# Recurrence of a hybrid kernel: VectorE's scan inputs ahead of sorting and placing, and GpSimd's scatters one step later

## What is computed

```python
# recurrence, for the normalised x of a batch; in time t the state is h
k = x @ Wz + bz
z = sigmoid(k)                                   # keep = 1 - z
h[t] = keep[t] * h[t-1] + z[t] * g(x @ Wh + bh)  # the reference does it in logs
out = layernorm(h) * gamma + beta + x
# mixture of experts, for the normalised rows xf
probs = softmax(xf @ router_w.T)
topv, topi = top_k(probs, 2)
y = sum over the two chosen experts of share * expert(xf)
```

## Time and profile before

| what | value |
|---|---|
| median of three runs | 1427.84 us (1422.67, 1434.9, 1427.84) |
| span of the profiled execution, first to last instruction | 1524.2 us |
| recurrence in that execution, first memset to the next stage's first load | 973.4 to 1238.1 us |
| roots of steps 8 to 35 (start to start) | 1025.27 to 1208.60 us |

### The profile page before, as it was taken

The page is one execution under the profiler, slowest core; times in us unless marked ns, Lnnn a source line. Parts: engine busy times, 40 slices in busy tenths (PEclk is TensorE's granted clock), DMA queues, the critical chain, the costliest instruction groups (busy, mean ns, idle before and its releaser), DMA issues. The chain is left out here.

```text
span 1524.2 us, 38116 instructions
## 1 busy us (share of the span) xinstructions
PE 1216.6 (80%) x11689; PEld 1017.3 (67%) x11689; DVE 1144.1 (75%) x3833; ACT 967.7 (63%) x2078; POOL 991.9 (65%) x1131
## 2 busy tenths in 40 slices
PE   5889999999999999973788888577787449888850
PEld 3667777777777777753788888455566348788850
DVE  5489999999999999965566665488888546666638
ACT  3588888888888888851555544277777435455420
POOL 4346688888888888777355665237777835666530
PEclk9699999999999999995799997588878669999955
DMA  7211111111111111123222222112222122222228
GB/s 199 86 46 46 48 60 60 60 60 60 59 60 60 60 60 60 39 93 83 73 86 86 81 85 68 49 49 83 73 83 69 45 68 84 86 84 84 77 83 277
DMA packets 99443, 117.19 MB, mean 77 GB/s; under 512 B 17784, under 2 KB 79792, under 8 KB 99248
## 3 DMA queue, kind: packets, MB, share of 16 engines
q1 hardware_dynamic: 70560, 73.57, 16.3%
q0 software_dynamic: 16896, 35.16, 6.8%
q10 hardware_dynamic: 11792, 6.05, 1.4%
HBM read 47.56 MB, written 41.51 MB: 58 GB/s over the span
## 5 line engine op out<-in xcount | busy, mean ns | idle before, releaser
L1153 DVE TENSOR_TENSOR ebuf<-score_banks,region 128x768 f32<-128x768 f32 x256 | 243.6, 951 | 18.8 <-PE score_banks L862 13.1
L1402 ACT ACTIVATE region<-ebuf 128x768 f32<-128x768 f32 x256 | 215.9, 860 | 23.0 <-DVE ebuf L1153 23.0
L1380 ACT CAST copied<-max_banks 128x768 bf16<-128x768 f32 x251 | 201.9, 804 | 15.1 <-PE max_banks L850 12.5
L1842 POOL DMA_INDIRECT choice_rows<-second_yo,second_xg x136 | 133.1, 979 | 112.7 <-PE second_by L1880 69.3
L1842 POOL DMA_INDIRECT choice_rows<-first_yo,first_xg x136 | 130.7, 961 | 114.0 <-PE first_by L1880 65.9
L1694 POOL DMA_INDIRECT expert_rows<-d_rows,a_d_index x112 | 129.4, 1155 | 27.9 <-issue 17.2
L1918 ACT ACTIVATE second_silu<-second_bgu,second_biases 128x256 f32<-128x256 f32 (+1 forms) x144 | 61.0, 466 | 114.3 <-PE second_bgu L1871 66.7
L1918 ACT ACTIVATE first_silu<-first_bgu,first_biases 128x256 f32<-128x256 f32 (+1 forms) x144 | 61.9, 462 | 111.8 <-issue 83.6
L1954 DVE SCALAR_TENSOR_TENSOR second_hT<-second_bgu,second_biases,second_silu 128x256 f32<-128x256 f32 (+1 forms) x144 | 62.1, 464 | 70.3 <-ACT second_silu L1918 37.6
L905 PE MATMUL bankO<-region,vaug 128*32 128x256 f32 (+1 forms) x2048 | 111.1, 334 | 1.9 <-ACT region L1402 1.9
L853 PE MATMUL max_banks<-region_r 32*128 32x256 f32 x502 | 98.3, 388 | 11.9 <-DVE ebuf L1153 7.4
(11 more groups left out here) (369 smaller groups left out, 4531.6 us busy)
## 6 DMA issues: line engine op xcount, KB each, us to landing
region_r<-region_r SPq DMA_DIRECT2D x192, 128.0 KB
first_xg<-expert_rows SPq DMA_DIRECT2D x64, 132.0 KB
second_xg<-expert_rows SPq DMA_DIRECT2D x64, 132.0 KB
z_rows<-choice_rows SPq DMA_DIRECT2D x32, 256.0 KB
c_rows<-choice_rows SPq DMA_DIRECT2D x16, 512.0 KB
out<-xres ACTq DMA_DIRECT2D x16, 256.0 KB
choice_rows<-first_yo,first_xg POOLq DMA_INDIRECT x136
choice_rows<-second_yo,second_xg POOLq DMA_INDIRECT x136
```

What stands on the lines that cost most here:

```text
L1153: nc.vector.tensor_tensor(ebuf[:, half_of_ebuf(c, j), :, :], score_banks[:, :, 0:BK], bias32[:, plain(j), :], ALU.add).then_inc(scores_fre ...
L1380: nc.scalar.copy(copied[:, 2 * j:2 * j + 2, :], banks_of_max(c, j)[:, :, 0:BK]).then_inc(maxed_free, 1)
L1402: nc.scalar.activation(p32[:, j % 4, :, :], ebuf[:, half_of_ebuf(c, j), :, :], ACT.Exp).then_inc(exped, 1)
L1842: pool.indirect_dma_start(choice_dram, bass.IndirectOffsetOnAxis(ap=xg[:, i % G, t, E:E + 1].bitcast(I32), axis=0), yo[:, i % 4, t, :], No ...
```

## The change

In VectorE's step `values` comes right behind `statistics`, ahead of `sort`, `number` and `place`. In GpSimd's step the scatters of a group that is not late move by one step each: those of the first choices to the even step after the placing, those of the second choices to the odd step after that. The late groups keep theirs.

```diff
                     if norms(i):
                         statistics(i, q)
+                    if scans(i):
+                        valued = values(i - 2, q)
                     if chosen_in(i) is not None:
                         dve.wait_ge(d_logits_taken, 2 * chosen_in(i) + 2)
                         d.sort(ch, chosen_in(i))
                         d.number(ch, chosen_in(i)).then_inc(d_compared, 1)
                     if placed_in(i) is not None:
                         place(placed_in(i))
-                    if scans(i):
-                        valued = values(i - 2, q)
                     if norms(i):
                         shifts(i, q)
...
                     if i >= 8 and q == 0 and not d.late((i - 8) // 2):
-                        scatter((i - 8) // 2, 1)
-                    if placed_in(i) is not None:
-                        scatter(placed_in(i), 0)
-                        if d.late(placed_in(i)):
-                            scatter(placed_in(i), 1)
+                        scatter((i - 8) // 2, 0)
+                    if i >= 9 and q == 1 and not d.late((i - 9) // 2):
+                        scatter((i - 9) // 2, 1)
+                    if placed_in(i) is not None and d.late(placed_in(i)):
+                        for k in range(2):
+                            scatter(placed_in(i), k)
```

## The result

The changed kernel takes 1433.33 us (median of 20 runs, 1424.32 to 1442.33) against 1426.28 us of the kernel before (20 runs, 1418.6 to 1434.9). The ratio is 1.0055, 95% interval 1.0037 to 1.0072: slower, clear of noise. The forecast was 1424.0 us.

The account below looks back on a forecast made before the run. GpSimd was taken to bound nearly every recurrence step. Terms -7.5 (scatters), +1.0 (root), -0.8 (step 7) and +3.5 (end) gave -3.8 us, so 1427.84 became 1424.0 us, range 1411 to 1434.

Parts of the forecast that it names:

- What bounds the stage: In the recurrence, GpSimd with four scatters and a root bounds nearly every step; VectorE is close behind.
- Moving the scatters: Steps 8 to 34: GpSimd no longer waits for indices ahead of first scatters, steps fall to 6.51 us, 7.5 us gained.
- What `values` does to the root: Roots running beside `values` on VectorE take slightly longer, between 0 and 1.9 us in all, taken as 1.0 us lost.
- VectorE's saving: `values`, 0.79 us, fits into VectorE's wait for the ranks, so VectorE's pair of steps is 12.5 us against GpSimd's 13.0.
- Step 7: Step 7 has no scatters any more and goes from 7.37 to 6.6 us, 0.8 us gained.
- The end: Four more scatters behind the last root cost 0 to 5.05 us, taken as 3.5.
- The changed place of the wait: Rival, chance 0.14: GpSimd's idle moves from scatter to root, only step 7 gains, the tail costs 5.05 us; 1432 us.
- VectorE the bound: Rival, chance 0.24: VectorE bounds the recurrence in the runs, so `values` in its waits gains 12 us; say 1417 us.
- the signs: Listed signs of being wrong: 6.8 us steps with idle ahead of roots, roots of 1.7 us, GpSimd idle every step, cheaper tail.
- Its 1%: For the whole kernel, about 1% (14.3 us) is what a measurement can tell from no change.
- The mutual hold: Rival, chance 0.04: each root is held while both `values` instructions run, 0.79 us a step, 20.5 us in all; 1443.5 us.

Follow-up runs that it names:

- the earlier trace: The profile of the kernel before that was shown ahead of the prediction, with no edit; its span was 1524.2 us.
- `values` alone: `values` moved ahead, scatters left in their old steps, against the kernel before: 1434.15 us, ratio 1.0061.
- the second profile: The kernel before profiled once more without an edit, for an execution near its median: 1423.95 us.
- the row sum: The changed kernel with one row sum of 256 elements (one SBUF input) put ahead of the scan: 1423.50 us, ratio 0.9983 to the kernel before.
- scatters alone: Scatters moved by a step, `values` left behind sorting and placing, against the kernel before; also called scatters only: 1429.55 us, ratio 1.0022.

## Why the prediction was wrong

**What bounds the stage**: right. From root 8 to root 35 GpSimd stands for nothing but the 0.2 to 0.3 us of issue, before (0.8 us for indices, 0.2 for an argument) and after (0.7 us ahead of roots).

**Moving the scatters, 7.5 us gained**: the step that failed. It took 6.51 us as what a step costs once GpSimd waits for nothing, from step 8 of the earlier trace rows, and counted the 8.0 us of the earlier trace rows as gained. By itself the move gained 2.7 us between these roots (183.75 to 181.04), and together with `values` it lost 1.1. For that 6.51 holds a first scatter of 1.03 us only because VectorE was late there and began its scan behind it, 0.49 us after the scatter of 1026.82:

```profile
1027.31 0.69 DVE L2194 TENSOR_TENSOR_SCAN z_h<-z_keep,z_val 128x256 f32<-128x256 f32 x1
```

The two profiles of the kernel before show both states of one stretch: in the first, GpSimd stands 8.0 us for indices and its first scatters take 1.039 us on average; in the second it stands 0.8 us and they take 1.376, which is 27 x 0.337 = 9.1 us more; from root 8 to root 35 it is 183.3 and 183.8 us. So a wait that goes comes back inside the scatters. The prediction asked what would be late next and found nothing, since it looked at waits and not at the length of what GpSimd does. That VectorE waited 14.3 us for ranks in the first profile and 6.3 in the second goes with TensorE's granted clock in the stretch, 0.83 and 0.92 (both mixes of the two levels); that the clock is the cause was not tried, and the changed kernel's VectorE, at 0.82, still waits 14.4 us for roots. The span of the first profile, 96 us above the median, was noted in the prediction and not drawn on.

**What `values` does to the root, 1.0 us**: near for the root (on average 1.399 us after 1.367, 27 x 0.032 = 0.9), but the larger part was put at nothing. The prediction says itself that `values` runs beside a scatter in a step that GpSimd bounds, and gives that no price and no reason for none. What pays is the scatter that begins while `values` or the scan runs: 1.15 for 0.96, and 1.45 for 1.03 us. By moving `values` to the end of the statistics the change puts it beside the fourth scatter in 18 of the 27 steps, where sorting and placing had stood: 27 x (1.089 - 0.959) = 3.5 us. With `values` alone it is 23 steps and 4.3 us. Between the roots of the changed kernel that makes +3.5 and +0.9, less 2.6 for first scatters, 11 of which no scan held, and 0.8 for indices: 1.0, where 1.1 was measured and -6.5 forecast.

**VectorE's saving**: worth nothing, since in the second profile VectorE already waits for the roots, 15.0 us before and 14.4 after at L2183. It is then on time, and starts its scan some 0.09 us ahead of the scatter. In the earlier trace rows it came late, behind the root and the scatter, and the scatters of the earlier trace rows took 1.03. The same group in the first profile shows it:

```profile
L2183 DVE SCALAR_TENSOR_TENSOR z_shift<-z_mv,z_rs 128x6 f32<-128x6 f32 x27 | 4.2, 157 | 1.8 <-POOL z_rs L2271 1.8
```

**Step 7, -0.8**: measured -0.9. **The end, +3.5 of at most 5.05**: a little above the upper bound, 5.3. The chains of VectorE and SP that seemed to hold the stage in the earlier trace rows were slow in that execution only; in the other nine profiles SP's four blocks take 4.4 to 4.6 us.

**The rivals.** The changed place of the wait (0.14) gives 1432 us, 1.3 below the measured time, and that is luck: its count of the two ends was right, but no idle time moved ahead of the roots (0.7 us there); what kept the roots where they were is the longer scatters. Nor is VectorE the bound (0.24): it waits for the roots. Steps of 6.85 us in which GpSimd stands nowhere are none of the signs that the prediction listed. Its 1% as the least change that can be told was too coarse: 20 runs of each kernel tell 0.55%. The mutual hold got 0.04, and is nearest to what happened: its kind was right, its place (the root) and its price (0.79 us a step) were not. The Trainium skill, "SBUF — State Buffer", section "Who interferes with whom", says that a VectorE instruction with two SBUF inputs contends with a GpSimd instruction that reads SBUF, that one with a single SBUF input outside certain modes does not, and that the one that starts first has the port while the other is blocked in full. The runs agree in the first two, and in half of the third: the scan holds the scatter (1.45), the row sum does not (1.03), and a scan that begins 0.03 us behind the scatter does not either; but that scan is not blocked, it keeps its 0.69 us. The held scatter follows the end of what holds it: between roots 8 and 35 of the ten profiles 109 first scatters begin behind the start of a scan that still runs, and every one of them ends 0.83 to 0.86 us behind that scan's end, whether 0.37 or 0.62 us of it were left. Of the blocked time not all is lost: the scatter of 1005.71 loses 0.42 us of the 0.60 that the scan still runs. Why 0.18 us are free no run here tells.

The parts don't add up exactly: values alone +0.61%, scatters alone +0.22%, both +0.55%. The intervals, about a quarter of a per cent each way for the parts, leave room for that. The rows of scatters and stretches are of one execution of each kernel. In the profiled execution of the changed kernel some steps take 6.4 us with a first scatter of 1.03, others 7.0 with one of 1.45; why the steps of one execution differ so was not tried.

## What to carry to other kernels

When the bounding engine is GpSimd with indirect DMAs, look at the duration of each, not only at the waits between them: one that is longer than its fellows at the same place of every step points at the VectorE instruction that began just ahead of it. Starting a two-operand VectorE instruction a little later, behind the scatter, can be worth more than taking work off VectorE. Before a wait is counted as a gain, ask whether it was also what kept two engines out of each other's way, and take a second profile when the span of the first lies well above the median of the runs.

## What the runs showed of the hardware that was not expected

Three memsets of 128 x 32 elements, 0.17 us together, make the kernel before 0.45% faster (0.9955), by moving a scan from 0.08 us ahead of an indirect DMA to 0.05 us behind it. The hold goes one way here: the scan that begins second keeps its duration beside the scatter, 0.67 us against 0.68 when it began first. Starts that nearly coincide can go either way: in scatters only, the scatter of 1121.91 begins 0.04 us behind an L2189 and keeps its 1.03, while the L2189 takes 0.49 instead of 0.42. A two-operand instruction with one operand in PSUM does not hold a scatter (0.96), one of the same size with both in SBUF does (1.15).
